# A decoder layer with a selective scan: TensorE waits for each product with C by itself instead of for two at once

## The reference

```python
proj = jnp.einsum('blh,ph->blp', x, in_proj_w)
h_in, gate = jnp.split(proj, 2, axis=-1)
...
dA = jnp.exp(dt[..., None] * A[None, None])
dBx = (dt * uT)[..., None] * Bm[:, :, None, :]
_, hstates = jax.lax.associative_scan(combine, (dA, dBx), axis=1)
y = jnp.einsum('blin,bln->bli', hstates, Cm) + D * uT
y = y * jax.nn.silu(gate)
return jnp.einsum('bli,hi->blh', y, out_proj_w)
```

## Time and profile before

| | |
|---|---|
| median of 3 runs | 5232.07 us (5219.92 to 5234.57) |
| the profiled execution, its own time | 5223.07 us |
| its span, first to last instruction | 5221.2 us |
| mean granted TensorE clock | 0.976 |
| PE, DVE, ACT, POOL busy | 90%, 88%, 84%, 83% of the span |
| the product's additions, line 1128 | 8192 matmuls, 1096.3 us busy |
| the products on POOL, line 313; on DVE, line 1492 | 1280, 1703.3 us; 768, 527.7 us |

### The profile page before, as it was taken

The page is one execution under the profiler, slowest core; times in us unless marked ns, Lnnn a source line. Parts: engine busy times, 40 slices in busy tenths (PEclk is TensorE's granted clock), DMA queues, the critical chain, the costliest instruction groups (busy, mean ns, idle before and its releaser), DMA issues. The chain is left out here.

```text
span 5221.2 us, 141020 instructions
## 1 busy us (share of the span) xinstructions
PE 4699.5 (90%) x51012; PEld 3370.9 (65%) x51012; DVE 4617.0 (88%) x6307; ACT 4384.6 (84%) x9314; POOL 4311.4 (83%) x3466
## 2 busy tenths in 40 slices
PE   4789999999999999999999999999999999998976
PEld 3566666666666666666666666666666666666653
DVE  2889999999999999999999999999999999998961
ACT  3788889888898888889988898988889888888862
POOL 2888888888898888888888888888889888888860
PEclk8899999999999999999999999999999999999986
DMA  3202222212222211222221222221222221122200
GB/s 118 74 29 79 70 76 78 78 41 74 72 71 78 78 58 56 72 74 78 74 78 36 78 69 78 78 78 41 73 72 70 78 78 57 57 72 71 66 13 7
DMA packets 114706, 350.31 MB, mean 67 GB/s; under 512 B 13056, under 2 KB 14848, under 8 KB 113920
## 3 DMA queue, kind: packets, MB, share of 16 engines
q1 hardware_dynamic: 114048, 341.51, 20.2%
HBM read 323.64 MB, written 17.83 MB: 65 GB/s over the span
## 5 line engine op out<-in xcount | busy, mean ns | idle before, releaser
L304 POOL TENSOR_TENSOR ring<-du,bc 128x512 f32<-128x512 f32 x2048 | 2594.2, 1284 | 622.0 <-PE ps L1128 408.5
L472 ACT ACTIVATE ps<-delta,a_neg 128x254 f32<-128x254 f32 x4096 | 1767.9, 467 | 38.3 <-DVE ring L1508 25.5
L313 POOL TENSOR_TENSOR ring<-ring,bc 128x512 f32<-128x512 f32 x1280 | 1703.3, 1337 | 109.1 <-DVE ring L1508 106.7
L1508 DVE TENSOR_TENSOR_SCAN ring<-ps,ring 128x512 f32<-128x512 f32 x1280 | 1549.1, 1215 | 102.6 <-ACT ps L472 83.6
L1128 PE MATMUL ps<-ident,ring 128*128 128x128 f32 x8192 | 1096.3, 278 | 46.8 <-POOL ring L313 41.6
L1128 PEld LDWEIGHTS ps<-ident,ring 128*128 128x128 f32 x8192 | 926.1, 142 | 253.2 <-issue 169.7
L1508 DVE TENSOR_TENSOR_SCAN ps<-ps,ring 128x512 f32<-128x512 f32 x768 | 933.6, 1216 | 116.5 <-ACT ps L472 109.7
L1492 DVE TENSOR_TENSOR ring<-ps,bc 128x512 f32<-128x512 f32 x768 | 527.7, 687 | 15.7
L627 ACT ACTIVATE probs_mem<-ps 128x768 f32<-128x768 f32 (+1 forms) x512 | 445.6, 911 | 105.7 <-PE ps L1072 99.5
L1196 PE MATMUL ps<-w_in,xt_a 128*128 128x256 f32 x2048 | 474.3, 386 | 16.1 <-DVE hc L1623 8.1
L1176 PE MATMUL ps<-xt_a,w_in 128*128 128x256 f32 x2048 | 472.0, 384 | 7.6 <-DVE hc L1623 4.1
(11 more groups left out here) (144 smaller groups left out, 6915.0 us busy)
## 6 DMA issues: line engine op xcount, KB each, us to landing
w_in<-in_w_in SPq DMA_DIRECT2D x256, 512.0 KB, 3.7
bc<-bc_rows SPq DMA_DIRECT2D x256, 512.0 KB, 5.1
x_new<-in_x SPq DMA_DIRECT2D x32, 512.0 KB, 7.4
x_res<-in_x SPq DMA_DIRECT2D x32, 512.0 KB, 6.7
enc<-in_ctx SPq DMA_DIRECT2D x64, 256.0 KB, 3.1
out<-x_att SPq DMA_DIRECT2D x32, 512.0 KB, 2.8
w_outp<-in_w_outp SPq DMA_DIRECT2D x1, 2048.0 KB, 8.1
bc_rows<-bc_sb SPq DMA_DIRECT2D x32, 32.0 KB, 1.5
```

Of the source, the lines that this page charges most:

```text
L304: nc.gpsimd.tensor_tensor(ring[:, s % RING, :].rearrange("p (n t) -> p n t", n=2), du[:, q % 2, (ic % 2) * NT:(ic % 2 + 1) * NT].rearrange ...
L313: nc.gpsimd.tensor_tensor(ring[:, s % RING, :], ring[:, s % RING, :], bc[:, s % RS, 2:4, :].rearrange("p a t -> p (a t)"), ALU.mult).then_ ...
L472: nc.scalar.activation(ps[:, s % DAR, (n % 2) * NT:(n % 2 + 1) * NT].rearrange("p (b t) -> p b t", b=GB)[:, :, 1:T], delta[:, ic, :].rearr ...
L1508: nc.vector.tensor_tensor_scan(state, ps[:, s % DAR, :], ring[:, s % RING, :], 0.0, ALU.mult, ALU.add).then_inc(h_done, 1)
```

## The change

The two waits that stood in front of a pair, one for each product counter and both up to step `s`, become one wait in front of each step's four additions, for that step's own product and on the counter of the engine that makes it. The additions, their order and their signals stay.

```diff
-                reached(pe, hcd_done, g * NDC + dvc(s + 1))
-                reached(pe, hcp_done, g * NPC + s + 1 - dvc(s + 1))
                 for t in range(s + 1 - BATCH, s + 1):
+                    if t in DVE_C:
+                        reached(pe, hcd_done, g * NDC + dvc(t + 1))
+                    else:
+                        reached(pe, hcp_done, g * NPC + t + 1 - dvc(t + 1))
                     for n in range(2):
                         for b in range(GB):
                             last = nc.tensor.matmul(ps[:, PS_Y, b * T:(b + 1) * T],
```

## The result

The changed kernel took 5296.77 us (median of 6 runs, 5277.29 to 5303.83) beside 5233.32 us for the kernel before (6 runs, 5219.92 to 5246.48) on the same chip: 1.0106 of its time, with a 95% interval of 1.0087 to 1.0124. That is 63 us slower, where the prediction had 6 us less. The profiled execution has a span of 5293.0 us, 71.8 us more than before, and 141116 instructions, 96 more. In the changed file the additions are line 1130 (1128 before), DVE's product 1494 (1492), its scan 1510 (1508), its maximum 1532 (1530), `h_in` 1178 (1176), `gate_in` 1198 (1196), the output projection 1160 (1158); lines of ACT and POOL keep their numbers.

The account below looks back on a forecast made before the run. The prediction saw a closed loop of hand-overs with no engine full. Gains of 5.1 (iterations 1 to 30), 0.5 (first) and 0.4 us (last) sum to 6.0 us less: 5226 us against 5232.07, with 8 in 10 for 5205 to 5246.

Parts of the forecast that it names:

- waits removed and added: PE's additions: two waits per pair before and after, 2048 in all; no matmul, load, signal or DMA added.
- the two signs named for being wrong: Met waits lengthening a pair's eight additions to 1.07 us or more, or the iteration shrinking by 0.5 us or more.
- The rival of the other side: Middle wait breaks PE's stream at each pair's fifth load, up to 0.05 us 1024 times: 5258 us; 10 in 100.
- The cost of a met wait: Between a pair's fourth and fifth loads, an already met wait costs 0; upper bound 0.05 us per pair, 51 us.
- Pair 37: Additions of step 36 move into the wait, PE 0.44 us sooner, all returned at line 1054: taken as 0.
- Pair 59: PE goes on 0.39 us sooner, of which ACT's copy gains 0.17 us in each of 30 iterations: 5.1 us.
- The ends: First iteration, 11 waits for POOL's product, gains 0.5 us; last iteration, step 60 moving into the wait, gains 0.4 us.
- POOL's slots: POOL's wait for ring slots in front of line 304 was to stay near 408.5 us; splitting moves nothing there.

Follow-up runs that it names:

- experiment 3: The changed kernel with the head of PE's loop at slot 200 of its block instead of 0: 5247.94 us, ratio 1.0008 to the kernel before.
- experiment 7: The kernel before with the change in pairs 51 and 59 alone, both POOL/POOL pairs: 5309.59 us, ratio 1.0136.
- experiment 6: The kernel before with the change in pair 59 alone, a POOL/POOL pair: 5236.29 us, ratio 1.0001.
- Experiment 1: The kernel before, but POOL/POOL pairs read both counts of hcp_done in front of the pair's first addition, no middle wait: 5313.06 us, ratio 1.0129.
- experiment 5: The kernel before with the change only in the 24 pairs per iteration that hold a DVE step: 5235.29 us, ratio 0.9998.
- experiment 12: The whole changed kernel with the head of PE's loop at slot 232 instead of 0: 5239.14 us, ratio 1.0004 to the kernel before.
- experiment 4: The changed kernel without waits of PE that an earlier wait of its own covers: 5307.73 us, ratio 1.0137 to the kernel before.
- experiment 2: The kernel before with the head of PE's loop at slot 16 instead of 0, no loop instruction changed: 5313.75 us, ratio 1.0144.

## Why the prediction was wrong

**The step that failed** is "waits removed and added". It counted waits on a queue ("two waits per pair before, two after") and found nothing new: "no matmul, load, signal or DMA is added". A wait on a count worked out from g is also a register instruction, unless that count has been worked out before. 16 of them were new in a body, and 13 packets of instructions with them. With the loop's head at slot 200 or 232 the same instructions cost nothing that the ratios show (1.0008 and 1.0004). At slot 0 they pushed the closing branch over the end of a block, by 14 instructions, which cost 63 us. The rows that would have warned were in the profile of before: 416 packets on the instruction queue, PE's records per body at 6654 of 6656, and the loop's head fixed at slot 0. I read neither the queue nor the branch, and what decided was none of the engines' waits for one another. Neither of the two signs named for being wrong came: the eight still take 1.04 us, and no iteration of the loop shrank. The price of the return stood in no term, so no sign could point at it.

The Trainium skill (Runtime: NRT & Kernel Launch, section Instruction fetch mechanics) says that an engine's instructions are fetched in blocks of 256, that a taken branch to a block that isn't held forces a fetch before execution goes on, and that crossing a block is "mostly hidden". The packets of 16384 bytes and the branches of 4.5 to 6.6 us without the hint agree with the first two. So does experiment 3 with the third: its body crosses into a 27th block at no cost. But when the crossing comes just ahead of the branch, the return costs 5.61 us in the mean with the hint given (experiment 7, against 0.36 in experiment 6).

**The rival of the other side had the sign, not the cause.** It said that the waits' counts are "computed from g inside the loop", and priced that at up to 0.05 us in each of 1024 pairs, in PE's stream of matmuls. Experiment 1 has the loss without a middle wait, experiment 5 has 24 middle waits per iteration without a loss. The right observation was put in the wrong place. Its 5258 us and the chance of 0.10 for slower were both too low.

**The cost of a met wait was right as far as it can be seen.** I took 0 from line 1093. Experiments 3, 5, 12 give 1.0008, 0.9998, 1.0004. Only against the kernel before at slot 200 is there more, 1.0021, some 11 us (an estimate), and whether that is the waits or the two chips is open. In the changed trace, 798 of the 832 pairs read have 0.109 us between the fourth and the fifth matmul, the spacing they have anywhere, and eight take 1.04 us as before.

**Pair 37 was right.** Changed kernel, g = 19, timeline:

```profile
3190.71 1.53 PE L1130 MATMUL ps<-ident,ring 128*128 128x128 f32 x12
...
3191.77 1.47 DVE L1532 TENSOR_REDUCE nmax<-ps 128x8 f32<-128x1280 f32 x1
3192.46 0.42 PEld L1130 LDWEIGHTS ps<-ident,ring 128*128 128x128 f32 x4 [0.45 <-POOL ring L313]
3192.46 0.66 PE L1130 MATMUL ps<-ident,ring 128*128 128x128 f32 x4 [0.21 <-POOL ring L313]
...
3193.29 0.32 PE L990 MATMUL ps<-band,ident 32*128 32x320 bf16 x4 [0.18 <-DVE nmax L1532]
...
3196.70 0.55 PE L1054 MATMUL ps<-ident,nmax 128*128 128x128 f32 x3 [0.83 <-DVE nmax L1532]
```

The first twelve are pair 35 and step 36. Then PE stands 0.21 us, where it stood 0.65, and the last four follow. Line 990 now has a wait of its own, 0.18 us for DVE's maximum, and line 1054 waits 0.83 us instead of 0.65. Of the 0.44 us, 0.18 and 0.18 are in these two waits. Over 265 to 5110 us the stops at the additions are

```profile
PE ps L1130 <- POOL ring L313: 6.7, 31, 0.3
```

13.0 us less than in the earlier trace rows, of which nothing arrives: the second halves keep their 154.7 us.

**Pair 59 was mis-sized: 0.17 us per iteration, and it is 0.** The mistake was in the working, not in the chip. Line 1112's two matmuls were said to "take 0.43 us of PE each" and PE to be free at 3034.09 to 3034.13. From 3033.66 two of them end their spacing at 3033.66 + 0.86 = 3034.52, which is just when line 1128 began. PE stood for nothing there; the 0.64 us that the loads waited were covered. After (g = 19, second iteration of a body):

```profile
3238.69 1.02 PE L1112 MATMUL ps<-o_sb,w_ct 128*128 128x512 f32 x2
...
3239.55 1.04 PE L1130 MATMUL ps<-ident,ring 128*128 128x128 f32 x8
...
3240.42 3.62 PE L1198 MATMUL ps<-w_in,xt_a 128*128 128x256 f32 x16
...
3243.46 0.63 ACT L534 ACTIVATE soft<-soft 128x512 f32<-128x512 f32 x1
...
3244.13 0.59 ACT L586 COPY gate_t<-ps 128x512 f32<-128x512 f32 x1
```

The additions begin 0.86 us after line 1112, as before, and ACT's copy 0.67 us behind the start of line 534, where the earlier trace rows had 0.71. The waiting load is gone and what follows moved by 0.04 us at most. The run with pair 59 alone (1.0001, 0.9987 to 1.0016) agrees, but can't tell 5 us from nothing; the rows decide.

**The ends were right.** In the first iteration the waits for POOL's product did not fall, 19.3 us in 11 and now 20.8 in 12. But the iteration itself, from its first scan to the next one's, became shorter: 147.1 us where it was 147.8, and so in every trace but that of experiment 4. The seven whose pairs wait as before have 147.8 to 148.0, the changed kernel at its three slots 147.1 to 147.2, the partly changed ones 147.3 to 147.4. That is 0.7 us, where 0.5 was taken. In the last iteration, step 60 does move into the wait:

```profile
5133.40 0.66 PE L1130 MATMUL ps<-ident,ring 128*128 128x128 f32 x4 [1.05 <-POOL ring L313]
```

The stop of 1.39 us became 1.05. The output projection behind it begins 3.98 us after the start of line 1112 in front (5129.92 to 5133.90), where it was 4.47 (5055.04 to 5059.51): 0.49 us sooner, where 0.4 was taken. No measurement of the time could tell either gain from none.

**POOL's slots.** They were to stay near 408.5 us; they rose to 450.9. That goes with the returns and not with the split waits: experiment 2, with the waits of before, has 448.1, and the changed kernel at slot 200 has 428.4.

## What to carry to other kernels

When an edit touches a loop on the chip, count every instruction that it adds to each engine's body, the register operations for computed waits too, and see where in its block of 256 the closing branch then falls; a branch in the last quarter of its block cost 0.36 us here, one in the first 30 slots 3 to 6 us in the mean, with a stretch at half clock behind it. A loss that sits in every n-th iteration belongs to the loop, not to the edited lines: compare iterations with each other before lines with lines. And a load's wait under a running matmul is no stop of PE: take the stop from the matmul's start and the spacing of those in front of it.

## What the runs showed of the hardware that was not expected

- A taken branch of PE took 0.36 us, or up to 6.6, by its place in its block of 256 and by the hint; two instructions in a body of 6656 decided it (5236 or 5310 us).
- The same slot did not give the same price: at slot 13 the means were 4.32, 5.52 and 5.69 us in three kernels, and one branch of 13 at slot 61 took 5.36 us beside twelve under 1.7. Each long branch ended 2.3 to 2.8 us after the start of a packet; why that packet starts sooner or later is open.
- A stop of PE of 1.88 us was followed by about 3 us at a granted clock of 0.52, and eight matmuls that took 3.60 us at full clock took 5.39.
- A wait taken out of the program need not take an instruction with it: the three kinds of wait left out in experiment 4 made a body only 8 records shorter.
- The whole change at a harmless slot is worth nothing that these runs can measure (1.0008 and 1.0004, with 1 in both intervals). No version was found that is clearly faster than the kernel before: its own head at slot 200 gave 0.9987, 0.13% less, in one comparison; the changed kernel at slot 200 does not show such a gain.
